# Forming Q1, K1, V1 and the suffix sums in a row's own softmax units instead of one row ahead

## What is computed

```python
# branch 1, causal, weights 1 - tanh^2, its projections named Q1, K1, V1 below
q, k, v = (proj(Wq), proj(Wk), proj(Wv))
pressure = jnp.einsum('bhid,bhjd->bhij', q, k) * scale
pressure = jnp.where(causal, jnp.float32(-10000.0), pressure)
energy = (pressure - phase_threshold) / tau
attn = 1.0 - jnp.tanh(energy) ** 2
attn = attn / (jnp.sum(attn, axis=-1, keepdims=True) + 1e-06)
out = jnp.einsum('bhij,bhjd->bhid', attn, v)      # then @ Wo.T -> s
# branch 2, softmax attention on rmsnorm(xn) (Q2, K2, V2), then experts
attn = jax.nn.softmax(scores, axis=-1)
X = X + ctx @ wo
h2 = rmsnorm(X, norm2_w)
combine = ...                                     # top 2 of 8 experts
eout = jnp.einsum('etf,efd->etd', jax.nn.silu(gate) * up, e_down)
# X + shared expert + combined experts, silu of it -> g
x = x + s * g
```

## Time and profile before

| | |
|---|---|
| median of 3 runs | 1096.43 us (1095.84 to 1101.96) |
| the profiled execution: its own time | 1097.14 us |
| its span in the trace | 1095.4 us |
| PE busy | 990.9 us, 90% |
| DVE busy | 831.4 us, 76% |
| ACT busy | 646.8 us, 59% |
| POOL busy | 351.2 us, 32% |
| granted TensorE clock, mean over the span | 0.982 |
| start, until unit 2 of row 0 | 58 us |
| one row in the middle (unit 2 of row 3 at 450.5, of row 4 at 581.6) | 131.1 us |
| DMA | 81.83 MB, mean 75 GB/s |

### The profile page before, as it was taken

The page is one execution under the profiler, slowest core; times in us unless marked ns, Lnnn a source line. Parts: engine busy times, 40 slices in busy tenths (PEclk is TensorE's granted clock), DMA queues, the critical chain, the costliest instruction groups (busy, mean ns, idle before and its releaser), DMA issues.

```text
span 1095.4 us, 18252 instructions
## 1 busy us (share of the span) xinstructions
PE 990.9 (90%) x6763; PEld 467.3 (43%) x6784; DVE 831.4 (76%) x1684; ACT 646.8 (59%) x882; POOL 351.2 (32%) x211
## 2 busy tenths in 40 slices
PE   4489999899998999889998999989999899988997
PEld 1123464245542455324652346523554245532464
DVE  6885977869776888759878598795977779773962
ACT  3569724786258842698336972379624785258731
POOL 4702443033520355105530154203352033610032
PEclk9589999999999999999999999999999999999999
DMA  7350561023700435105331055211471033600020
GB/s 231 71 109 22 111 169 34 21 55 80 190 20 12 99 93 132 30 2 130 112 83 30 2 130 143 51 31 30 101 181 24 21 79 83 163 20 2 1 79 10
DMA packets 60392, 81.83 MB, mean 75 GB/s; under 512 B 8560, under 2 KB 47728, under 8 KB 57296
## 3 DMA queue, kind: packets, MB, share of 16 engines
q1 hardware_dynamic: 56544, 75.61, 28.3%
q10 hardware_dynamic: 3760, 5.05, 1.4%
HBM read 52.98 MB, written 27.39 MB: 73 GB/s over the span
## 4 chain that ended last, share of the span: by engine, by line
PE 53%; DVE 25%; ACT 12%; issue 4%; DMA 2%; SPq 1%; ACTq 0%; POOL 0%; DVEq 0%; POOLq 0%
PE O L1156 11%; DVE nmax L758 10%; DVE PT L813 9%; PE O L1139 7%; ACT PT L613 7%; PE S L1172 6%; PE S L1174 5%; PE S L1173 5%; PE S L1112 4%; PE M L1075 3%; PE M L1054 2%; PE M L1080 1%; PE O L1075 1%; SPq L368 1%; DMA stackQ<-mTZ 1%
## 5 line engine op out<-in xcount | busy, mean ns | idle before, releaser
L613 ACT ACTIVATE PT<-S 128x1024 f32<-128x1024 f32 (+1 forms) x448 | 417.0, 967 | 113.7 <-PE S L1112 108.7
L813 DVE SCALAR_TENSOR_TENSOR PT<-PT 128x768 f32<-128x768 f32 (+1 forms) x192 | 213.4, 1163 | 101.0 <-ACT PT L613 101.0
L758 DVE TENSOR_REDUCE nmax<-M 128x1 f32<-128x512 f32 x329 | 218.2, 684 | 43.2 <-PE M L1075 28.3
L1139 PE MATMUL O<-PT,V 128*32 128x256 f32 (+3 forms) x2816 | 246.5, 430 | 0.0
L494 POOL TENSOR_TENSOR PT<-PT,CB 128x1024 f32<-128x1024 f32 x56 | 133.6, 2392 | 261.2 <-DVE PT L951 146.9
L646 ACT ACTIVATE PT<-S 128x1024 f32<-128x1024 f32 x72 | 73.9, 1027 | 241.4 <-PE S L1174 241.4
L479 POOL TENSOR_TENSOR split<-split,parts 128x512 f32<-128x512 f32 x30 | 90.9, 3029 | 372.0 <-ACT parts L573 372.0
L1112 PE MATMUL S<-stackQ,stackK 64*128 64x512 bf16 (+3 forms) x1024 | 166.3, 347 | 9.5 <-DMA stackQ<-mTZ 5.3
L758 DVE TENSOR_REDUCE nmax<-O 128x1 f32<-128x512 f32 x183 | 125.1, 684 | 36.5 <-PE O L1075 17.6
L1172 PE MATMUL S<-h2hi,wgu_hi 128*128 128x512 f32 x288 | 148.7, 516 | 4.3 <-DVE PT L951 4.2
L1156 PE MATMUL O<-PT,wdn 128*128 128x512 f32 x288 | 142.9, 595 | 0.9
(11 more groups left out here) (198 smaller groups left out, 1044.5 us busy)
## 6 DMA issues: line engine op xcount, KB each, us to landing
CB<-scrC SPq DMA_DIRECT2D x64, 256.0 KB, 5.6
stackQ<-scrQ SPq DMA_DIRECT2D x30, 384.0 KB, 5.5
stackK<-scrK SPq DMA_DIRECT2D x30, 384.0 KB, 6.3
scrQ<-parts SPq DMA_DIRECT2D x32, 192.0 KB, 3.3
scrK<-parts SPq DMA_DIRECT2D x30, 192.0 KB, 5.9
scrQ<-parts SPq DMA_DIRECT2D x32, 128.0 KB, 3.4
scrK<-parts SPq DMA_DIRECT2D x30, 128.0 KB, 5.2
KX<-scrK SPq DMA_DIRECT2D x14, 192.0 KB, 3.4
```

The lines of the kernel that those rows point to most:

```text
L613: a.activation(PT[:, n % SLOTS, 2 * q * w:2 * q * w + 2 * w].rearrange("p (r n) -> p r n", r=2), S[k][:, :].rearrange("p (r n) -> p r n", ...
L758: v.tensor_reduce(nmax[:, h % 2, h // 2, t:t + 1], M[k][:, :], AX.X, ALU.max, negate=True).then_inc(m_read[k], 1)
L813: v.scalar_tensor_tensor(p, p, 1.0, p, ALU.subtract, ALU.mult).then_inc(weighed, 1)
L1139: last = t_.matmul(O[k][32 * q:32 * q + VW, i0:i1], V[:, j, 4 * g + q, :], PT[:, n % SLOTS, w * q + at:w * q + at + i1 - i0], start=(j == ...
```

## The change

`Q1`, `K1` and `V1` leave the set `AHEAD`: they are no longer formed for the next row, but for the row itself, in units 2, 4 and 6. There they may use all three M buffers (`THREE`). The suffix goes from expert 0 to unit 9, ahead of `maxT_Z`. For that, `corr` gets memory of its own. GpSimd splits Q1 and K1 right at the start of its row's work, ahead of the tile sums of V1. SP stores Q1's parts before it waits for Y's rows, loads Q1's stack behind them, then stores K1's parts, writes Z's rows, and loads K1's stack. In the start of the program, Q1, K1 and V1 fall away.

```diff
-PLACES[9] += ["maxT_Z"]
+PLACES[9] += ["suffix", "maxT_Z"]
+for n, name in ((2, "Q1"), (4, "K1"), (6, "V1")):
+    PLACES[n].append(name)
...
-PLACES[25] += ["Q1"]
 PLACES[26] += ["h2T"]
-PLACES[27] += ["logits", "K1"]
-PLACES[EXPERT] += ["suffix"]
+PLACES[27] += ["logits"]
...
-PLACES[EXPERT + 4].insert(2, "V1")
...
-AHEAD = {"xnT", "hT", "Q2", "K2", "V2", "Q1", "K1", "V1", "maxT_X", *MAX["X"], "maxT_W", *MAX["W"]}
+THREE = {"Q1", "K1", "V1"}
+AHEAD = {"xnT", "hT", "Q2", "K2", "V2", "maxT_X", *MAX["X"], "maxT_W", *MAX["W"]}
...
-            k = min(range(3 if name[0] == "max" else 2), key=lambda b: last[b])
+            k = min(range(3 if name[0] == "max" or name in THREE else 2), key=lambda b: last[b])
...
-        corr = h2T[:, :].rearrange("p (t d) -> p t d", t=NT)
+        corr = sb("corr", [128, NT, D])
...
-                for run in ("Y", "Z"):
-                    wait_apart(sp, *read(u, "maxT_" + run))
-                    maxima_rows(run)
+                store_parts("Q1", 2, it)
+                wait_apart(sp, *read(u, "maxT_Y"))
+                maxima_rows("Y")
...
+                load_stack(sp, "Q1", it)
+                store_parts("K1", 3, it)
+                wait_apart(sp, *read(u, "maxT_Z"))
+                maxima_rows("Z")
+                load_stack(sp, "K1", it)
...
-                wait_apart(pool, *read(ROWS[it - 1] if it else FIRST, "V1"))
+                for name in ("Q1", "K1"):
+                    for _step in split_steps(u, name, it, True):
+                        pass
+                wait_apart(pool, *read(u, "V1"))
...
-                    if following and e < 3:
-                        for _step in split_steps(u, ("Q1", "K1")[e - 1], it + 1, True):
-                            pass
...
-                    if e == 0:
-                        take(u, it, "suffix")
                         combine(it)
...
+                if k == 2:
+                    pe.wait_ge(o_read[1], it * O_USES[1] + 1)
```

More of the change, by code:

```diff
@@ L96 @@
 PLACES[END] += ["maxT_W", "outL"]
-START = PLACES | {16: ["hT"], 18: ["K2", "xnT"], 19: ["V2", "V1"],
-                  EXPERT + 4: [w for w in PLACES[EXPERT + 4] if w != "V1"],
+START = PLACES | {16: ["hT"], 18: ["K2", "xnT"], 19: ["V2"],
                   EXPERT + 5: [w for w in PLACES[EXPERT + 5] if w not in MAX["W"]],
                   EXPERT + 6: MAX["W"][:2] + ["maxT_X"] + MAX["W"][2:], EXPERT + 7: [], EXPERT + 8: []}
-AHEAD = {"xnT", "hT", "Q2", "K2", "V2", "Q1", "K1", "V1", "maxT_X", *MAX["X"], "maxT_W", *MAX["W"]}
+THREE = {"Q1", "K1", "V1"}
+AHEAD = {"xnT", "hT", "Q2", "K2", "V2", "maxT_X", *MAX["X"], "maxT_W", *MAX["W"]}
 class Uses:
@@ L359, in restack @@
                     store_part(sp, name, i, part)
+            def restack(name, i, bt):
+                store_parts(name, i, bt)
                 load_stack(sp, name, bt)
@@ L385, in prepare @@
                     restack("K2", 1, bt)
-                    for k in range(2):
-                        wait_apart(sp, s_full[k], it * S_USES + UNITS)
                     spread_weights(u, it)
-                    restack("Q1", 2, bt)
-                    restack("K1", 3, bt)
                 for run in ("X", "W"):
@@ L393, in prepare @@
                     maxima_rows(run)
[L394 to L403, removed]
             def spread_weights(u, it):
@@ L499, in row @@
                 g.tensor_scalar(x1[:, :, :], xn[:, :, :], 1.0, None, ALU.mult).then_inc(carried, 1)
-                wait_apart(pool, *read(ROWS[it - 1] if it else FIRST, "V1"))
+                for name in ("Q1", "K1"):
+                    for _step in split_steps(u, name, it, True):
+                        pass
+                wait_apart(pool, *read(u, "V1"))
                 if it > 0:
-                    wait_apart(pool, *full(ROWS[it - 1] if it else FIRST, "suffix"))
+                    wait_apart(pool, *full(ROWS[it - 1], "suffix"))
                 g.tensor_tensor(VS[:, 1, :], V1c[:, 2, :], V1c[:, 3, :], ALU.add).then_inc(v_summed, 1)
@@ L566, in projection @@
                 scale = {"Q2": {"scale": HD ** -0.5}, "Q1": {"scale": qs1[:, :]}}.get(name, {})
+                if name == "Q1":
+                    act.wait_ge(scaled, 1)
                 if i >= 2:
@@ L667, in _ @@
                 for name in FIRST.places[n]:
[L668 to L671, removed]
+                    if name == "V2":
+                        act.wait_ge(v_set, 1)
                     if name != "maxT_W":
@@ L909, in row @@
                         take(u, it, name)
-                    if it == 0 and n == 10:
-                        constants()
                     if n == 0 and it > 0:
@@ L918, in row @@
                             maxima_parts(u, run)
+                    if it == 0 and n == 8:
+                        constants()
                 if following:
@@ L1214, in work @@
                     if name == "Q1":
-                        wait_read(u, "xnT", name)
+                        pe.wait_ge(*read(ROWS[it - 1] if it else FIRST, "xnT"))
                     w, src = (w2s, hT) if name[1] == "2" else (w1s, xnT)
-                    projected(u, name, w[:, 0 if name[0] == "Q" else 1, :], src)
+                    projected(u, it, name, w[:, 0 if name[0] == "Q" else 1, :], src)
                 elif name in ("V2", "V1"):
-                    projected_v(u, name, (w2s if name == "V2" else w1s)[:, 2, :], hT if name == "V2" else xnT)
+                    projected_v(u, it, name, (w2s if name == "V2" else w1s)[:, 2, :], hT if name == "V2" else xnT)
                 elif name[0] in ("oT2", "oT1"):
@@ L1235, in work @@
                     if name == "proj2":
-                        projected_v(u, name, w2s[:, 3, :], ctxT)
+                        projected_v(u, it, name, w2s[:, 3, :], ctxT)
                     else:
-                        projected(u, name, w1s[:, 3, :], ctxT)
+                        projected(u, it, name, w1s[:, 3, :], ctxT)
                 elif name == "h2T":
```

22 lines of the change are left out of this document (12 added, 10 removed).

## The result

The changed kernel takes 1103.5 us (19 runs, 1099.04 to 1106.69), the kernel before 1098.5 us (19 runs, 1095.84 to 1102.06). The ratio is 1.0040 with an interval of 1.0028 to 1.0052: slower by a little, well within the 1% that the forecast called no change. The profiled execution took 1102.83 us (span 1100.8) against 1097.14 (1095.4), 5.4 us more in the span. The forecast was +1.0 us, so 4 to 5 us of the difference do not stand in its sum.

The account below looks back on a forecast made before the run. Bound: DVE's maxima up to softmax unit 9, then ACT; DVE late in the causal units; PE from expert 2. Rows 0 to 6 -0.1 us each, row 7 +1.7, together +1.0 on 1097.14: 1098 us, range 1085 to 1110.

Parts of the forecast that it names:

- Q1, K1 and V1 in units 2, 4 and 6: Softmax units: each projection makes DVE's maxima 0.7 us late, 2.1 us a row in all.
- The suffix in unit 9: Unit 9: its 1.48 us on PE replace a 1.34 us wait for mhZ; about 0.2 us a row lost.
- K1's removal counts 0: Units 25 and 27: PE and ACT do less for Q1 and K1, but DVE is the limit; gain 0.
- the router's chain 0.9: DVE's chain L818 to L951, freed of GpSimd's splits, shortens from 3.69 to 2.76 us; 0.9 us a row gained.
- V1 out of expert 4: Expert 4, where PE is the limit: without V1, 0.9 us a row gained.
- Transfers: SP's queue: K1's stack lands with 2 us of slack before unit 16; cost 0, up to 3 us.
- Row 7: Last row, with no next row to prepare: pays 2.3 us, gains 0.6 us, +1.7 us.
- GpSimd beside DVE: Softmax units: splits beside DVE's reductions, which never contend, cost 0; if they did, 3.6 us a row.
- The start: Program start: Q1, K1 and V1 lay in shadows of other waits, so dropping them gains 0.
- Y's rows and K1's stack: Rival, chance 0.13: SP's in-order queue makes these transfers late; 1.6 us in each of 8 rows, 1111 us.
- the insertions: Rival, chance 0.12: in the softmax units only buffer latency shows, loss 0.8 instead of 2.3 us; 1086 us.
- gains do not arrive: Rival, chance 0.15: among the experts, V1's 0.9 us becomes a wait, perhaps the suffix's 0.6 too; 1104 to 1109 us.

Follow-up runs that it names:

- e4: The changed kernel with Q1, K1 and V1 over 128 of 512 tokens only; profiled once: units 2 to 15 still +2.05 us against the kernel before.
- e2: The kernel before, with only GpSimd's splits of Q1 and K1 put behind the weights of experts 1 and 2; 1098.27 us, ratio 0.9997.
- e6: The changed kernel with the suffix back in expert 0, so only Q1, K1 and V1 moved; profiled once, span 1100.5 us.
- e3: The kernel before with the edit of e2 and the suffix in unit 9 with its own corr; 1092.27 us, ratio 0.9947.
- e5: The kernel before with only the suffix moved to unit 9, with its own corr; profiled once, span 1095.0 us.
- e7: e3 with Q1 and K1, still a row ahead, in units 23 and 25 instead of 25 and 27; 1091.99 us, ratio 0.9946.
- e8: e7 with V1 in unit 6 of its own row, as in the change; 1089.48 us, ratio 0.9918.
- e9: The kernel of e6 (changed kernel, suffix back in expert 0), now timed; 1102.28 us, ratio 1.0039.
- e10: The kernel of e4 (changed kernel, Q1, K1 and V1 over 128 of 512 columns), now timed; 1097.67 us, ratio 0.9988.
- e11: The changed kernel with two idle projections added for PE in units 23 and 25, results thrown away; 1102.06 us, ratio 1.0028.

## Why the prediction was right, and where its steps were wrong

The forecast of "within 1%" and the range held, and the balance within a row was right to 0.1 us: -0.1 measured, as forecast. The steps behind it were not all right.

*Q1, K1 and V1 in units 2, 4 and 6: right in mechanism, slightly too high.* 0.5, 0.65 and 0.64 us instead of three times 0.7, with DVE idle 0.56 us behind Q1. e4 shows that for Q1 and V1 it is the buffer: the third one had hidden this latency. For K1 it shows that the projection's own time counts (0.13 us were left at a quarter of the width), as the prediction had it, in which K1 delays the score half and pair behind it.

*The suffix in unit 9: mis-sized.* Forecast 0.2, measured 0.63. The step took the 1.34 us wait for mhZ in row 3 as that of every row. In row 5 of before it reads:

```profile
734.26 0.23 PE L1086 MATMUL M<-identb,mhZ 128*32 128x128 bf16 x1 [0.98 <-DVE mhZ L768]
```

The seven other rows have unit 9 at 3.06 us, row 3 alone at 3.42. The suffix occupies PE from 474.39 to 476.12, 1.73 us, in the place of 0.98, and the difference, 0.75, lies near the 0.63. Had another row been read, the term would have been 1.48 - 0.98 = 0.5. The stretch came to 39.43 us in row 3, against 39.6 forecast, by luck: the loss of 2.55 us was larger than forecast, and row 3 of before was 0.36 us longer than its like.

*K1's removal counts 0, the router's chain 0.9: the split between them was wrong, the sum nearly right.* Experts 0 to 2 gained 1.76 us where 1.5 were forecast (0.9 for the chain and 0.6 for the suffix). But e2 shows that the chain alone is worth 0 and that K1 in unit 27 was the wait behind it. The step "DVE is the limit there, so I count 0" looked at DVE's load and not at what comes to L951 second.

*V1 out of expert 4: right*, -0.88 against -0.9. *Transfers: right for K1's stack*, no wait for it at unit 16, *but Z's rows were not in the sum*. Their four DMAs take SP 2.76 instead of 2.64 us (row 3, at 478.40 and, before, at 474.55), and unit 11 is 0.12 us longer. Both come with Q1 and K1 in their own row, whose stores and loads now stand beside them in SP's queue: e6, which has no suffix in unit 9, shows them, and e3, e5, e7 and e8 do not. Why the DMAs take longer is not shown. In row 4 Z's rows were 1.2 us late besides. *Row 7: right*, 1.9 against 1.7.

*GpSimd beside DVE: right.* In the changed kernel the first split step of Q1 takes 1.16 us beside DVE's maxima; before, in the causal units, the same step took 8.19 us:

```profile
515.74 8.19 POOL L479 TENSOR_TENSOR split<-split,parts 128x512 f32<-128x512 f32 x1 [11.24 <-ACT parts L573]
```

```profile
457.55 1.16 POOL L476 TENSOR_TENSOR split<-split,parts 128x512 f32<-128x512 f32 x1 [4.79 <-ACT parts L570]
```

The mean DVE reduction is 684 ns in both kernels. The Trainium skill says in "SBUF — State Buffer", section "Who interferes with whom", that a reduction on trn2 never contends with GpSimd; the trace agrees with these 684 ns.

*The start: missed.* It gave 1.5 us in the profiled execution, forecast 0. With Q1, K1 and V1 out of it PE's first maxima come at 27.43 instead of 28.63 us. But the start of single executions of one kernel differs as well (0.8 us between e6 and e9, 3.4 between e4 and e10), so how much of this is the change's stays open.

*The clock: not in the sum at all.* This is the one step that failed in effect: removing PE work from units in which DVE is the limit was costed at 0. In the stage itself it is 0, in undisturbed rows to 0.01 us. But it leaves PE busy for 7.83 instead of 8.88 of 10.0 us, and the granted clock then fell more often, at a price of up to 3.2 us each time here and 4.4 us in e6. The runs show that the lower median clock comes with this removal (e9, e10) and goes when PE is given work there (e11). They do not show at which activity it falls: the rows 0, 1, 3, 4 and 5 of the changed kernel have the same 7.82 or 7.83 us in that place and kept their clock there, before kept it over 10.0 us with PE busy 7.51 (599.6 to 609.6, row 4), and some falls stood elsewhere, as the one at 614.0 in unit 11 of row 4.

The rivals: none came. Y's rows and K1's stack were in time, the gains among the experts arrived, and the insertions were not absorbed. The time lies at 1103.5 nevertheless, near that of the rival "gains do not arrive", for another reason: a time alone would have seemed to confirm it.

## What to carry to other kernels

Work taken from an engine that waits is not free if that engine is TensorE: read its busy time in the stretch and the granted clock of many executions, and look for rows that are longer than their neighbours. Before a gain is put down to one of several things that end in the same wait, ask which comes second; of the cases run here only those without all three gave 1.76 us. And read a wait in several rows before it becomes a term: the one row chosen was the exception. The best version found, e8, moves V1 and the suffix as the change does, and Q1 and K1 only two units forward, so that TensorE keeps this work in the causal units.

## What was not expected of the hardware

TensorE fell to half clock in the middle of a kernel in which it is 91% busy, for 3.4 us twice and 10.2 us once, ahead of which it had been busy for 78 to 84% of 10.0 us. In row 4 the fall came in a wait of 2.05 us; in rows 2 and 6 no idle time in these 10.0 us was longer than 1.32 us. The one of row 6:

```profile
911.53 0.29 PE L1103 MATMUL S<-never,identb 128*128 128x128 bf16 x2 [1.31 <-ACT PT L610]
```

The Trainium skill describes in "TensorE: Matmul & The Clock Gate", section "A second HAM failure mode: psum-queue depth-cycling", that many short idle times between groups of matmuls can make the clock swing between its two levels. The trace agrees only in part: the fall of row 6 has two idle times ahead of it, 1.31 and 0.86 us, but five other rows have the same busy time there and kept their clock. The price depends on length and place: 0.5 us for 3.4 us where another engine is the limit (row 6), 3.2 us for 10.2 us that reach into expert 0's matmuls (row 2).

Apart from these stretches and from row 4's wait for Z's rows, executions agree to 0.01 us in nearly every unit, between kernels too. So a difference of 0.1 us a row can be read from two single traces, when rows with a lower clock are set aside, though the timed runs used here would not have shown it.
